# Attention row sums inverted as 128 rows of four instead of one row set of 512, by way of transfers, two half heads ahead of their use

## The reference

```python
x = x + 0.5 * ffn(layernorm(x))     # shared SwiGLU + 8 experts, top 2
x = x + attention(layernorm(x))
x = x + 0.5 * ffn(layernorm(x))     # the same weights again
```

```python
# 16 query heads, 4 key/value heads, head size 32, rotary embedding
scores = einsum('bhqd,bhkd->bhqk', q, k) * 32 ** -0.5
attn = softmax(scores, axis=-1)
out = einsum('bhqk,bhkd->bhqd', attn, v)
return einsum('bsh,oh->bso', out.reshape(b, s, 512), Wo)
```

## Time and profile before

| | us |
|---|---|
| median of 3 runs | 1814.74 (1812.5 to 1818.36) |
| the profiled execution's own time | 1814.38 |
| its span | 1812.6 |
| PE, DVE, POOL, ACT busy | 1635.8, 1065.2, 917.9, 656.7 |

### The profile page before, as it was taken

The page is one execution under the profiler, slowest core; times in us unless marked ns, Lnnn a source line. Parts: engine busy times, 40 slices in busy tenths (PEclk is TensorE's granted clock), DMA queues, the critical chain, the costliest instruction groups (busy, mean ns, idle before and its releaser), DMA issues.

```text
span 1812.6 us, 23865 instructions
## 1 busy us (share of the span) xinstructions
PE 1635.8 (90%) x8356; PEld 1164.7 (64%) x8356; DVE 1065.2 (59%) x1470; ACT 656.7 (36%) x974; POOL 917.9 (51%) x757
## 2 busy tenths in 40 slices
PE   6999999999988888888878788787899999999997
PEld 5677899999776633333333333321677889889985
DVE  5554222222777789988988888877655432222226
ACT  4422232232332344544544444454343122223221
POOL 3115764236677565655656556563040629550745
PEclk9999999999989989988889888898999999999998
DMA  9215544333723200100000000000310535432527
GB/s 342 86 55 198 212 169 146 114 122 114 233 75 90 63 18 18 27 23 23 19 19 18 18 19 18 1 21 4 142 52 1 206 150 182 164 136 74 177 82 244
DMA packets 67838, 175.66 MB, mean 97 GB/s; under 512 B 10768, under 2 KB 11664, under 8 KB 65424
## 3 DMA queue, kind: packets, MB, share of 16 engines
q1 hardware_dynamic: 54896, 100.48, 17.1%
q0 software_dynamic: 12832, 73.67, 11.5%
HBM read 102.29 MB, written 55.84 MB: 87 GB/s over the span
## 4 chain that ended last, share of the span: by engine, by line
PE 58%; DVE 21%; issue 7%; DMA 7%; ACT 3%; POOL 2%; SPq 1%; DVEq 0%; POOLq 0%; ACTq 0%
PE PS L1118 9%; PE PS L1120 9%; PE PS L1119 9%; DVE rL L1925 8%; PE PS L1351 5%; PE PS L1332 4%; PE PS L1381 4%; DMA xn<-x_routed 3%; DVE nmf_later L1902 3%; DMA xs<-x_routed 2%; DVE nmf_first L1902 2%; PE PS L1255 2%; PE PS L1260 2%; PE PS L1258 2%; PE PS L1257 2%
## 5 line engine op out<-in xcount | busy, mean ns | idle before, releaser
L1606 ACT ACTIVATE PT<-PS 128x1024 f32<-128x1024 f32 x256 | 258.0, 1024 | 241.2 <-PE PS L1351 239.6
L1351 PE MATMUL PS<-QS,KS 98*128 98x512 f32 x512 | 194.4, 466 | 94.6 <-DVE nmf_later L1902 67.7
L1351 PEld LDWEIGHTS PS<-QS,KS 98*128 98x128 f32 x512 | 95.2, 212 | 246.7 <-DVE nmf_later L1902 147.1
L950 POOL TENSOR_TENSOR added<-PT 128x1024 f32<-128x1024 f32 x60 | 148.0, 2466 | 204.0 <-ACT PT L1606 204.0
L1365 PE MATMUL PS<-PT,V 128*32 128x512 f32 x1024 | 229.1, 663 | 0.0
L1925 DVE RECIPROCAL rL<-OT 32x512 f32<-32x512 f32 x64 | 214.2, 3347 | 12.5 <-ACT OT L1615 10.6
L1902 DVE TENSOR_REDUCE nmf_later<-PS 128x1 f32<-128x1024 f32 x160 | 192.7, 1218 | 33.8 <-PE PS L1332 31.4
L1972 POOL TENSOR_TENSOR W<-raw,W 128x544 fp32r<-128x544 f32 x144 | 190.0, 1352 | 1.5
L1332 PE MATMUL PS<-KS,QS 96*128 96x512 f32 x512 | 182.7, 441 | 4.6 <-ACT PT L1606 2.3
L1869 DVE TENSOR_TENSOR thid<-thid,PS 128x352 f32<-128x352 f32 x78 | 40.6, 521 | 245.9 <-ACT thid L1537 245.9
L953 POOL TENSOR_TENSOR added<-added,PT 128x1024 f32<-128x1024 f32 x60 | 143.9, 2398 | 49.1 <-ACT PT L1606 46.8
(11 more groups left out here) (197 smaller groups left out, 3918.7 us busy)
## 6 DMA issues: line engine op xcount, KB each, us to landing
raw<-ffn_w POOLq DMA_DIRECT2D x18, 2176.0 KB, 10.3
y_routed<-ytile SPq DMA_DIRECT2D x78, 256.0 KB, 2.2
xn<-x_routed SPq DMA_DIRECT2D x40, 256.0 KB, 3.4
x_routed<-xq SPq DMA_DIRECT2D x1, 9984.0 KB, 29.5
xs<-x_routed SPq DMA_DIRECT2D x38, 256.0 KB, 3.4
QS<-later_hi SPq DMA_DIRECT2D x112, 64.0 KB, 2.0
raw<-ffn_w SPq DMA_DIRECT2D x6, 768.0 KB, 9.6
raw<-ffn_w SPq DMA_DIRECT2D x16, 272.0 KB, 4.1
```

Of the source, the lines that this page charges most:

```text
L950: e.tensor_tensor(to, PT[:, (u + 1) % PTBUF, :], PT[:, (u + 2) % PTBUF, :], ALU.add).then_inc(done.sem, 1)
L1351: mm = e.matmul(PS[:, i + j, :], KS[0:ROWS, b, g, kt * P:(kt + 1) * P], QS[n % 3][0:ROWS, h, hf * GRP:(hf + 1) * GRP], start=True, stop=True)
L1606: e.activation(PT[:, u % PTBUF, :], PS[:, i:i + 2, :].rearrange("p b n -> p (b n)"), ACT.Exp, scale=SCALE).then_inc(p_ready.sem, 1)
```

## The change

The reciprocal is taken out of its shape. `sums_out` (SP, unit 3) sends one row of 512 sums from OT to 128 partitions of four. `invert`, now in unit 1 of the next half head, has DVE invert 128 by 4 numbers; then SP writes the 512 inverses to DRAM, waits for that, and loads them back broadcast to 32 partitions of rL. `store_head` moves two half heads behind. OT and rL have two buffers each. At the end, `split_heads` of a tile waits only for its own half head, and the last invert and store stand behind the third tile's split.

```diff
+        if hh >= 1 and pair == 1:
+            work.append(("invert", hh - 1))
         if hh >= 0 and pair == 1:
             work.append(("values", hh, 1))
         if hh >= 0 and pair == 2:
-            if hh:
-                work.append(("store_head", hh - 1))
+            if hh > 1:
+                work.append(("store_head", hh - 2))
             work.append(("values", hh, 2))
         if hh >= 0 and pair == 3:
-            work.append(("invert", hh))
+            work.append(("sums_out", hh))
...
-    work.extend([("sum", hh), ("values", hh, 0), ("values", hh, 1), ("store_head", hh - 1), ("values", hh, 2),
-                 ("invert", hh), ("store_head", hh)])
+    work.extend([("sum", hh), ("values", hh, 0), ("invert", hh - 1), ("values", hh, 1), ("store_head", hh - 2),
+                 ("values", hh, 2), ("store_head", hh - 1), ("sums_out", hh)])
     work.append(("attention_end",))
+    last = [("invert", hh), ("store_head", hh), ("x_back",)]
...
+        if i == 2:
+            work.extend(last)
...
+            elif kind == "sums_out":                                  # SP
+                sp.wait_ge(ot_ready, hh)
...
+                e.dma_start(sums_in_rows[:, hh % 2, :],
+                            OT[SUMS:SUMS + 1, hh % 2, :].rearrange("o (p i) -> o p i", i=TPG)
+                            ).then_inc(sums_turned.sem, 16)
+            elif kind == "invert":                                    # SP
+                sp.wait_ge(inverted, hh)
...
+                e.dma_start(inverse_rows[hh % 2, :].rearrange("(p i) -> p i", i=TPG),
+                            inverses[:, hh % 2, :]).then_inc(inverse_out.sem, 16)
+                sp.wait_ge(inverse_out, hh)
...
+                e.dma_start(rL[SUMMED, hh % 2, :], inverse_rows[hh % 2:hh % 2 + 1, :].broadcast_to([QUARTER, GRP])
+                            ).then_inc(inverse_in.sem, 16)
             elif kind == "attention_end":                             # SP
-                heads_over(sp)
-                for g in ORDER:
+                sp.wait_ge(pv_done, last_half, 2)
+                g = ORDER[0]
+                e.dma_start(group_of_X(g), group_rows(x_home, g)).then_inc(x_back[g].sem, 16)
+            elif kind == "x_back":
+                for g in ORDER[1:]:
                     e.dma_start(group_of_X(g), group_rows(x_home, g)).then_inc(x_back[g].sem, 16)
...
-            elif kind == "attention_end":                             # PE; the same on ACT and DVE
-                heads_over(pe)
...
             elif kind == "split_heads":                               # ACT
                 t, = key
+                act.wait_ge(head_ready, half_of_tile(t))
+                act.wait_ge(pv_done, last_half, 2)
...
-            dve.wait_ge(inverted, hh)                                 # DVE, store_head
+            dve.wait_ge(inverse_in, hh)
...
             elif kind == "invert":                                    # DVE
-                dve.wait_ge(ot_ready, hh)
-                if hh:
-                    dve.wait_ge(head_ready, hh - 1)
-                e.reciprocal(rL[SUMMED, :], OT[SUMS:, :]).then_inc(inverted.sem, 1)
+                dve.wait_ge(sums_turned, hh)
+                if hh > 1:
+                    dve.wait_ge(inverse_out, hh - 2)
+                e.reciprocal(inverses[:, hh % 2, :], sums_in_rows[:, hh % 2, :]).then_inc(inverted.sem, 1)
```

More of the change, by code:

```diff
@@ L588, in macaron @@
     assert at >= slot_at[3] + slot_bytes
-    OT, behind = place("OT", (P, GRP), F32, at)
+    behind = at + QT * 2 * HD * 4
     nmf_first, behind = place("nmf_first", (P, REP, QT), F32, behind)
@@ L618, in macaron @@
     MT, at = place("MT", (QT, 2, 2, P), F32, at)
-    rL, at = place("rL", (P, GRP), F32, at)
+    OT, at = place("OT", (P, 2, GRP), F32, at)
+    rL, at = place("rL", (P, 2, GRP), F32, at)
+    sums_in_rows, at = place("sums_in_rows", (P, 2, TPG), F32, at)
+    inverses, at = place("inverses", (P, 2, TPG), F32, at)
     nmf_later, at = place("nmf_later", (P, 2 * REP, QT), F32, at)
@@ L623, in macaron @@
     PS = ctx.enter_context(nc.psum_tensor("PS", [P, 8, GRP], F32))
+    inverse_rows = nc.dram_tensor("inverse_rows", (2, GRP), F32, kind="Internal").ap()
     x_home = nc.dram_tensor("x_home", (TOK, D), F32, kind="Internal").ap()
@@ L687, in macaron @@
         signal(n) for n in ("ot_ready", "inverted", "parts_summed", "head_ready"))
+    sums_turned, inverse_out, inverse_in = (signal(n, 16) for n in ("sums_turned", "inverse_out", "inverse_in"))
     o_done, o_added = signal("o_done"), signal("o_added")
@@ L864, in macaron @@
                 a.plan(*key)
+        elif kind == "sums_out":
+            sums_turned.plan(*key)
         elif kind == "invert":
-            inverted.plan(*key)
+            for a in (inverted, inverse_out, inverse_in):
+                a.plan(*key)
         elif kind == "wo":
@@ L870, in macaron @@
         elif kind == "attention_end":
-            for g in range(NG):
+            x_back[ORDER[0]].plan()
+        elif kind == "x_back":
+            for g in ORDER[1:]:
                 x_back[g].plan()
@@ L973, in slots_over, with half_of_tile @@
         lane.wait_ge(down_done, 0, last_step, LATE * TPG + TPG - 1)
+    def half_of_tile(t):
+        b, hf = t // QT, t % QT // TPG
+        n = max(i for i, of in enumerate(KV_GROUPS) if of[0] == b)
+        return ((n + 1) * REP - 1) * 2 + hf
     def heads_over(lane):
@@ L1097, in sync_program @@
                 e.dma_start(woraw[:], wo[:, c, :]).then_inc(wo_in.sem, 16)
-            elif kind == "attention_end":
-                heads_over(sp)
-                for g in ORDER:
+            elif kind == "sums_out":
+                hh, = key
+                sp.wait_ge(ot_ready, hh)
+                if hh > 1:
+                    sp.wait_ge(inverted, hh - 2)
+                e.dma_start(sums_in_rows[:, hh % 2, :],
+                            OT[SUMS:SUMS + 1, hh % 2, :].rearrange("o (p i) -> o p i", i=TPG)
+                            ).then_inc(sums_turned.sem, 16)
+            elif kind == "invert":
+                hh, = key
+                sp.wait_ge(inverted, hh)
+                if hh > 1:
+                    sp.wait_ge(inverse_in, hh - 2)
+                e.dma_start(inverse_rows[hh % 2, :].rearrange("(p i) -> p i", i=TPG),
+                            inverses[:, hh % 2, :]).then_inc(inverse_out.sem, 16)
+                sp.wait_ge(inverse_out, hh)
+                if hh:
+                    sp.wait_ge(inverse_in, hh - 1)
+                if hh > 1:
+                    sp.wait_ge(head_ready, hh - 2)
+                e.dma_start(rL[SUMMED, hh % 2, :], inverse_rows[hh % 2:hh % 2 + 1, :].broadcast_to([QUARTER, GRP])
+                            ).then_inc(inverse_in.sem, 16)
+            elif kind == "attention_end":
+                sp.wait_ge(pv_done, last_half, 2)
+                g = ORDER[0]
+                e.dma_start(group_of_X(g), group_rows(x_home, g)).then_inc(x_back[g].sem, 16)
+            elif kind == "x_back":
+                for g in ORDER[1:]:
                     e.dma_start(group_of_X(g), group_rows(x_home, g)).then_inc(x_back[g].sem, 16)
@@ L1380, in store_head @@
             until_free(MISC)
-            e.matmul(PS[SUMMED, MISC, :], thirds[:], OT[0:SUMS, :],
+            e.matmul(PS[SUMMED, MISC, :], thirds[:], OT[0:SUMS, hh % 2, :],
                      start=True, stop=True).then_inc(parts_summed.sem, 1)
@@ L1611, in scalar_program @@
                 act.wait_ge(pv_done, hh, 2)
-                if hh:
[L1613 to L1617, removed]
+                if hh > 1:
+                    act.wait_ge(parts_summed, hh - 2)
+                    act.wait_ge(sums_turned, hh - 2)
+                e.activation(OT[:, hh % 2, :], PS[:, out_bank(n, hf), :], ACT.Copy).then_inc(ot_ready.sem, 1)
             elif kind == "split_heads":
@@ L1834, in store_head @@
             dve.wait_ge(parts_summed, hh)
-            dve.wait_ge(inverted, hh)
+            dve.wait_ge(inverse_in, hh)
             e.tensor_tensor(qtok[h * HD:(h + 1) * HD, t0:t0 + TPG, g * P:(g + 1) * P],
                             PS[SUMMED, MISC, :].rearrange("p (j n) -> p j n", n=P),
-                            rL[SUMMED, :].rearrange("p (j n) -> p j n", n=P), ALU.mult).then_inc(head_ready.sem, 1)
+                            rL[SUMMED, hh % 2, :].rearrange("p (j n) -> p j n", n=P), ALU.mult).then_inc(head_ready.sem, 1)
         for kind, *key in work:
@@ L1917, in vector_program @@
                 store_head(*key)
-            elif kind == "attention_end":
-                heads_over(dve)
             elif kind == "invert":
                 hh, = key
-                dve.wait_ge(ot_ready, hh)
-                if hh:
-                    dve.wait_ge(head_ready, hh - 1)
-                e.reciprocal(rL[SUMMED, :], OT[SUMS:, :]).then_inc(inverted.sem, 1)
+                dve.wait_ge(sums_turned, hh)
+                if hh > 1:
+                    dve.wait_ge(inverse_out, hh - 2)
```

(1 more changed line is left out.)

## The result

The changed kernel takes 1738.28 us (median of 4 runs, 1733.54 to 1743.56), where the kernel before took 1814.37: a ratio of 0.958, interval 0.954 to 0.962. That is 76.1 us less. The profiled execution, the shortest of the four, has a span of 1731.7 us, 80.9 less than the one before. The forecast was 1737.

A forecast was written before the change was run, and what follows sets the result against it. DVE and PE take turns, neither full, with the reciprocal on the path. Gains of 61 us (142 less 81 of stalls), 12 in the last group and 5 at the end make 78 off 1814.4: about 1737, range 1705 to 1765.

The forecast's parts named there:

- seven groups, if nothing waits: Attention before the last group: 55 half heads at 7.37 us plus extras make 420 us against 562, 142 less.
- stalls after queries: Half heads with place_queries: SP's twelve issues, 7.5 us, delay write, load and sums; 12 stalls of 6.7 us, 81 us.
- PE's idle time in one: In each stall after query transfers, PE's scores wait for banks behind DVE's late reciprocal: 5.0 us idle.
- the low clock after one: After each stall's idle time PE's clock stands at 0.50 for some 3.3 us, losing about 1.7 us.
- last group: Last attention group: PE's waits for DVE's sums shrink by 4 us for each of three, 12 us.
- last sums to first product: End: first output product about 7 us after PE's last sums, where it was 8.4.
- POOL's chain: Ordinary half head: POOL's chain for the third values round ends at 712.23, before PE comes at 712.6; 0.4 us left.
- the second rival: Half heads: PE cannot keep 7.37 us because POOL's chain and bank hand-over are tight; at 8.1 us, 1777 us; chance 0.17.
- The first rival: Half heads with query transfers: little or no stall of PE, 1655 us, or 1695 with half the stall; chance 0.19.
- The third: Rival on SP's transfers: SP becomes the bound; landings from 3.4 us on make it slower, 1902 us at 4.2; chance 0.12.
- The room of an ordinary half head: Ordinary half heads: the transfer chain can grow about 1.5 us unnoticed, SP's 1.1 and what PE has in hand.
- the rule on pieces under 512 bytes: Write of inverses to DRAM in 16-byte pieces: by this rule it would take longer than 2.2 us.

The follow-up runs named there:

- queries in two blocks: Changed kernel plus the register edit, SP's twelve query transfers sent as two blocks of six, each behind sums_out: 1659.62 us, ratio 0.9095.
- the edit alone: Changed kernel with only the register edit, two waits on a register's value taking max(value, 0) plus a constant: 1750.75 us, ratio 0.9585.
- the version that beats both: Queries in two blocks, all the last group's sums on DVE, and the end's last stores placed around the first tile's add: 1633.35 us, ratio 0.8987.
- longer chains: Changed kernel with register edit, inverses written again and waited for before the load: one more write 1762.11 us, ratio 0.9645; three more 1906.42 us, ratio 1.050.
- the run with three writes more: Changed kernel with register edit and three additional writes of the inverses, each waited for before load and sums_out: 1906.42 us, ratio 1.050.
- the kernel with the wide reciprocal: Changed kernel's order and two buffers with register edit, but reciprocal 32 by 512 straight from OT, without transfers of sums or inverses: 1847.92 us, ratio 1.0125.
- the old end: Changed kernel with register edit, last invert, last store and all of x's way back again ahead of the first split: ratio 0.9602.

## Why the prediction was right, step by step

| step | predicted | measured |
|---|---|---|
| seven groups, if nothing waits | 420 us, 7.64 a half head with all extras | 414.5, 7.54 (queries in two blocks) |
| stalls after queries | 12 | 12, and a small one |
| PE's idle time in one | 5.0 us | (46.4 - 1.3) / 12 = 3.8; 3.9 with the edit alone |
| the low clock after one | 1.7 us | 7.2 - 3.9 = 3.3 |
| seven groups | 61 less | 62.5 less |
| last group | 12 + 3.5 less | 15.1 less |
| last sums to first product | 1.2 less | 1.0 less |
| in all | 78 less | 76.1 less in the median, 80.9 in the profiled span |

The mechanism is the one foreseen, and the shares agree. Two terms of one step were wrong in opposite directions, and that their sum, 6.7 for 7.2, hid it is luck.

The idle time was too long by 1.1 us. The prediction added the 0.59 us of an issue to a landing of 2.05, but that landing is counted from the start of its issue, which is at 544.66 too. So it had 2.7 us from the write's issue to the load's; in the twelve stalls it was 2.0 in the mean, from 1.7 to 2.8 (687.32 - 684.74 = 2.6 in the one shown). From the load's issue to the next it was 0.37 us, not 0.7. Only the sums took what was reckoned, 2.7 us from issue to landing.

The price of the clock was half of what it is: I had read it from one place, after a wait of 3.90 us, where the clock was back in some 3 us; after 691.37 it was back only near 698. Across steps there was luck as well: the seven groups without waits are 5.5 us shorter than predicted, the stalls 4 us dearer.

POOL's chain, which I had seen 0.4 us clear, was clear: in the seven groups PE waited for nothing but the maxima. So the second rival had nothing. Only in the last group did PE wait for POOL's sums, 7.1 us in four waits, and DVE took these over in the version that beats both. The first rival, no stall, is what two blocks of six make of it: 1659.62 there, or 0.9095 x 1814.4 = 1650 on the scale of the kernel before, against 1655 predicted. The third was measured with longer chains. The room of an ordinary half head was put at 1.5 us, 1.1 of it SP's, and is larger: the sums landed 2.2 us ahead in the half head shown and about 3 in the median, with a chain longer by about a microsecond nothing but the stalls grew, and the run with three writes more speaks for 2.6 or more.

One attribution was wrong. I gave the last group's gain to the 3.35 us of reciprocal that go; the kernel with the wide reciprocal has the gain too, 18 us. The order is enough for it.

The DMA issues of the changed kernel (last column: median us from issue to landing), where `ytile` is the comparison of the earlier trace rows:

```profile
y_routed<-ytile SPq DMA_DIRECT2D x78, 256.0 KB, 2.2
rL<-inverse_rows SPq DMA_DIRECT2D x64, 64.0 KB, 2.9
sums_in_rows<-OT SPq DMA_DIRECT2D x64, 2.0 KB, 2.5
inverse_rows<-inverses SPq DMA_DIRECT2D x64, 2.0 KB, 1.7
```

About the rule on pieces under 512 bytes: the write of 128 pieces of 16 bytes to DRAM landed in 1.4, 1.7 and 2.9 us (least, median, most), the 256 KB of ytile in 2.2 in the median. The Trainium skill, DMA: Bandwidth & Descriptors, gives in its specifications 512 bytes as the least transfer for line rate, with read-modify-write below. At this size the trace shows no price for it in the time to landing. Nor did this write to DRAM land later than the sums, which go from OT to 128 partitions in pieces of the same size: 1.7 for 2.5 in the median.

## What to carry to other kernels

An operation whose time goes by columns per partition can be worth three transfers if they have a place to hide. Count that place on the queue that issues them, not only in microseconds of flight: here 7.5 us of unrelated issues in front cost 7.2 us each time. Split such blocks and put the pieces where the queue has nothing urgent behind it. And after a wait of PE price the clock too: here it was nearly as dear as the wait, 3.3 us for 3.9.

## What the runs showed of the hardware that was not expected

- How long the clock stays at 0.50, its lower level of 1.2 GHz, after an idle time of PE does not follow that time. After 3.90 us it was about 3 us, and after 3.94 us (at 800.26 in the changed kernel) the clock was at 1.00 again by 805. After 4.20 us it was nearly 7, and after only 3.24 us (at 985.56) the clock was 0.50 from 986 to 994 and 0.71 from 994 to 996. The mean over 12 stalls is 3.3 us lost.
- It fell with short waits too. In the seven groups before, no wait of PE for a maximum was longer than 2.2 us, and the mean clock was 0.89; without waits, with the queries in two blocks, it was 1.00.
- Runs of one kernel on one chip can lie apart by its clock: 1733.68 to 1750.42 us with the old end, with mean clocks from 0.949 to 0.961. It is not a mark of such waits: the changed kernel's runs lay within 10.0 us, those of the longer chains within 4.4 and 2.5, and those of three kernels without waits in the seven groups within 3.4, 7.0 and 10.1.
- Load and sums landed in 2.9 and 2.5 us (medians) behind one write, in 1.9 and 2.0 behind two. The cause is open.
